# A relational graph layer: rows made unique per tile of 128 edges instead of per pair of 256, with the two scatters of a pair one after the other

## The reference

```python
h = maximum(layernorm(x), 0)                      # no scale, no shift
S = h[src]                                        # one row for each edge
for r in (0, 1):
    t = relu(S @ W_rel[r].T + b_rel[r])
    msgs = where(rel == r, relu(t @ W_rel[r].T + b_rel[r]), msgs)
agg = segment_sum(msgs, dst, num_segments=50000)  # sum the messages of each destination
gates = agg @ W_ih.T + b_ih + b_hh                # i, f, g, o
c = sigmoid(i) * tanh(g)
hn = sigmoid(o) * tanh(c)
y = relu(hn @ W1.T + b1); y = relu(y @ W2.T + b2)
out = x + y @ W3.T + b3
```

## Time and profile before

| | us |
|---|---|
| median of 3 runs | 2441.94 |
| the profiled execution | 2442.41 |
| its span | 2440.8 |
| TensorE busy | 2137.6 (88%) |
| VectorE busy | 1795.0 (74%) |
| ScalarE busy | 1632.9 (67%) |
| GpSimd busy | 1188.1 (49%) |
| DMA, mean moved | 163 GB/s |

### The profile page before, as it was taken

One profiled execution on the slowest core, in us unless ns is written; L12 is line 12 of the kernel. 1 busy time (PEld: TensorE's weight loads), 2 busy tenths in 40 slices (PEclk: granted clock), 3 DMA queues, 4 the chain that ended last, 5 costly groups with the idle time before them and its releaser, 6 DMA issues.

```text
span 2440.8 us, 51857 instructions
## 1 busy us (share of the span) xinstructions
PE 2137.6 (88%) x14224; PEld 1411.5 (58%) x14225; DVE 1795.0 (74%) x4311; ACT 1632.9 (67%) x3366; POOL 1188.1 (49%) x917
## 2 busy tenths in 40 slices
PE   6858677767999999999999999999999999899997
PEld 5747565644665666665666566566666666444543
DVE  7547555555877778777777877787887877688885
ACT  2447555546777777777777777777777777566663
POOL 0037777775555555555555555555555543200000
PEclk7569988889999999999999999999999999999998
DMA  9946555556788888888888888888888887878786
GB/s 388 425 144 101 93 96 96 95 107 121 132 158 162 165 163 161 156 152 156 164 166 161 159 152 153 160 165 164 160 158 151 161 155 141 184 174 185 192 186 142
DMA packets 400606, 396.90 MB, mean 163 GB/s; under 512 B 263738, under 2 KB 343158, under 8 KB 394360
## 3 DMA queue, kind: packets, MB, share of 16 engines
q0 software_dynamic: 91200, 157.34, 39.8%
q1 hardware_dynamic: 306788, 238.12, 37.4%
q10 hardware_dynamic: 2516, 0.14, 0.1%
HBM read 185.88 MB, written 156.97 MB: 140 GB/s over the span
## 4 chain that ended last, share of the span: by engine, by line
PE 63%; issue 13%; ACT 10%; DMA 5%; POOL 4%; DVE 1%; SPq 1%; another core or an unknown queue 1%; POOLq 0%; ACTq 0%; DVEq 0%
PE bank L1472 30%; PE bank L1419 8%; PE bank L1486 5%; PE bank L1455 4%; PE bank L1438 4%; PE bank L1401 4%; DMA agg<-summed,scatter_idx 3%; PE bank L1511 3%; POOL agg L667 2%; POOL xg L651 2%; DMA a_lo<-row_lo 2%; ACT count_tmp L739 2%; ACT summed L727 2%; ACT tcell L786 2%; PE bank L1311 2%
## 5 line engine op out<-in xcount | busy, mean ns | idle before, releaser
L667 POOL DMA_INDIRECT agg<-summed,scatter_idx x400 | 638.2, 1596 | 676.5 <-DVE scatter_idx L1147 507.7
L1472 PE MATMUL bank<-a_hi,ihT 128*128 128x512 f16 x2400 | 716.8, 380 | 19.7 <-DMA a_lo<-row_lo 19.2
L651 POOL DMA_INDIRECT xg<-in_x,src_ring x400 | 453.6, 1134 | 269.1 <-DMA src_ring<-src_slot 137.3
L1472 PE MATMUL bank<-a_lo,ihT 128*128 128x512 f16 x1200 | 456.3, 380 | 0.0
L1472 PEld LDWEIGHTS bank<-a_hi,ihT 128*128 128x128 f16 x2400 | 234.4, 98 | 233.3 <-issue 26.6
L1438 PE MATMUL bank<-relT,h_hi 128*128 x1600 | 320.5, 275 | 0.0
L1419 PE MATMUL bank<-s_hi,relT 128*128 128x256 f16 x1600 | 305.3, 287 | 0.0
L1401 PE MATMUL bank<-ident,xn 128*128 128x128 f32 x800 | 132.1, 290 | 190.2 <-ACT xn L760 97.2
L675 POOL DMA_DIRECT2D y<-in_x x100 | 133.8, 1347 | 297.0 <-DVE y L1205 275.7
L1073 DVE SCALAR_TENSOR_TENSOR s_lo<-bank,s_hi 128x512 f16<-128x512 f32 x200 | 137.8, 689 | 161.4 <-ACT s_hi L733 140.3
L733 ACT ACTIVATE s_hi<-bank 128x512 f16<-128x512 f32 x200 | 119.7, 598 | 195.5 <-PE bank L1401 157.2
(11 more groups left out here) (197 smaller groups left out, 4718.9 us busy)
## 6 DMA issues: line engine op xcount, KB each, us to landing
agg_in<-agg SPq DMA_DIRECT2D x100, 512.0 KB
y<-in_x POOLq DMA_DIRECT2D x100, 512.0 KB, 6.5
out<-y SPq DMA_DIRECT2D x100, 512.0 KB
agg<-zeros SPq DMA_DIRECT2D x24, 2112.0 KB, 15.8
dst_ring<-dst_rows SPq DMA_DIRECT2D x200, 128.0 KB
xg<-in_x,src_ring POOLq DMA_INDIRECT x400
agg<-summed,scatter_idx POOLq DMA_INDIRECT x400
src_ring<-src_slot SPq DMA_DIRECT2D x200, 1.0 KB
```

The costliest lines, as they stand in the source:

```text
L651: nc.gpsimd.indirect_dma_start(out=xg[:, k.slot(8), t, :], out_offset=None, in_=x[:, :], in_offset=bass.IndirectOffsetOnAxis(ap=src_ring[: ...
L667: nc.gpsimd.indirect_dma_start(out=agg[:, :], out_offset=bass.IndirectOffsetOnAxis(ap=scatter_idx[:, k.slot(8), t:t + 1], axis=0), in_=sum ...
L1472: last = nc.tensor.matmul(N_C[c % 2][:, 0:UNIT], lhs, rhs, start=i == 0, stop=i == len(todo) - 1)
```

## The change

For pairs of the joint part (`both`) the indices are made unique within each tile and not within the pair. The block (tile 1 with 0) is no longer compared, counted or multiplied. The two scatters of such a pair may now hit the same row, so GpSimd issues the first, waits until it has landed, and then issues the second. One of the two gathers of the step is moved between them.

```diff
+        def rows_beside(k, t):
+            return slice(2 * t, 2 * t + 1) if k.both else same_span(t)
+        def all_rows(k):
+            return slice(0, SAME_BLOCKS, 2 if k.both else 1)
 ...
             def step(at):
-                k = at + 8
-                if k.within(PAIRS):
+                to_load, to_add = at + 8, at - 4
+                if to_load.within(PAIRS):
+                    k = to_load
                     pool.wait_ge(src_loaded[k.slot(8)], 16 * (k.turn(8) + 1))
                     wait_from(pool, normed, k.n - 7)
                     pool.sem_inc(gathers_cleared, 1)
-                    for t in range(2):  (the gather of tile t)
+                    gather(k, 0)
+                    if not to_add.both:
+                        gather(k, 1)
-                k = at - 4
-                if k.within(PAIRS):
+                if to_add.within(PAIRS):
+                    k = to_add
                     pool.wait_ge(idx_ready, k.n + 1)
 ...
                     pool.wait_ge(summed_ready, k.n + 1)
                     wait_from(pool, scattered, k.n * 32)
                     pool.sem_inc(scatters_cleared, 1)
-                    for t in range(2):  (the scatter of tile t)
+                    scatter(k, 0)
+                    if not k.both:
+                        scatter(k, 1)
+                if to_load.within(PAIRS) and to_add.both:
+                    gather(to_load, 1)
+                if to_add.within(PAIRS) and to_add.both:
+                    k = to_add
+                    pool.wait_ge(scattered, k.n * 32 + 16)
+                    pool.sem_inc(scatters_cleared, 1)
+                    scatter(k, 1)
 ...
@@ counts (ScalarE): both operands
-                        same_before[:, k.slot(2), same_span(t), :]
+                        same_before[:, k.slot(2), rows_beside(k, t), :]
@@ equal (VectorE)
-                                                       dst_ring[:, k.slot(2), 0:(t + 1) * P],
+                                                       dst_ring[:, k.slot(2), (t * P if k.both else 0):(t + 1) * P],
@@ equal_before (VectorE): all three operands
-                    same_before[:, k.slot(2), :, :]
+                    same_before[:, k.slot(2), all_rows(k), :]
@@ sums (TensorE)
-                    for t in range(to, 2):
+                    for t in range(to, to + 1 if k.both else 2):
```

More of the change, by code:

```diff
@@ L665, in step @@
                     pool.sem_inc(scatters_cleared, 1)
-                    for t in range(2):
-                        nc.gpsimd.indirect_dma_start(
-                            out=agg[:, :],
-                            out_offset=bass.IndirectOffsetOnAxis(ap=scatter_idx[:, k.slot(8), t:t + 1], axis=0),
-                            in_=summed[:, k.slot(4), t, :], in_offset=None, compute_op=ALU.add).then_inc(scattered, 16)
+                    scatter(k, 0)
[8 more added lines that the diff above has]
+                    scatter(k, 1)
                 k = at.unit - 3
@@ L1131, in equal_before @@
                     dve.wait_ge(same_ready, k.n + 1)
[L1132 removed]
+                    rows = all_rows(k)
+                    nc.vector.tensor_tensor(same_before[:, k.slot(2), rows, :], same[:, k.slot(2), rows, :], earlier[:, rows, :],
                                             ALU.mult).then_inc(same_before_ready, 1)
```

22 lines of the change are left out of this document (13 added, 9 removed).

## The result

The changed kernel takes 2535.0 us (median of 4 runs, 2521.6 to 2546.3), the kernel before on the same chip 2443.6: a ratio of 1.0376, 95% interval [1.0345, 1.0407], 92 us slower. The forecast was 2428 us with a range of 2402 to 2460. Both numbers lie outside it. The nearest of the rivals is D, 2538 us, to which I had given a chance of 0.10. The execution that was profiled is the longest of the four (2546.28 us, span 2544.6).

A forecast was written before the change was run, and what follows sets the result against it. The prediction took a path through ScalarE's copy L727, TensorE's register load and the transposes as the bound. Terms -5 - 15.6 + 0 + 2 + 4.4 = -14.2 us, from 2442.4 to 2428 us; range 2402 to 2460.

The forecast's parts named there:

- D: Joint part: GpSimd's loop of landings becomes the bound, 22.6 us for two steps, 2538 us; chance 0.10.
- What bounds the kernel: Joint part: the path runs from ScalarE's copy L727 through 1.64 us of register load to the transposes; sums lie beside it.
- rival A: TensorE in the joint part: the removed sum matmuls count in full, -31.5 us, giving 2401 us; chance 0.10.
- Steps 1 and 2: Joint pairs: two sum matmuls fewer on TensorE, -5 us; ScalarE's second count reading 128 columns, not 256, -15.6 us.
- Step 4: GpSimd's wait between a joint pair's scatters: loop of landings 20.2 us in two steps of 21.0, so cost 0.
- The sign of being wrong that I had given for D: GpSimd, joint part: in most steps the second scatter's landing and not scatter_idx releases GpSimd.
- Step 5: Joint part: y's load slides some 2.5 us, SyncE's queue absorbs it; 2 us in all.
- Step 6: Tail from 2096 us: later y and one more landing in front of it, +4.4 us, bounds 2.2 to 10.
- B: Joint part: y's slide reaches TensorE through SyncE's store, transpose and a_lo; 31 us, net +17, 2459 us; chance 0.15.
- C: Tail costs 10 us and the counts bring only part of 15.6: between -7 and 0, about 2439 us; chance 0.13.

The follow-up runs named there:

- experiment 11: Kernel before with the two sum matmuls across a joint pair's tiles left out, register load kept behind the sums; ratio 1.000 to the kernel before.
- experiment 9: Kernel before with TensorE's register load of the relations moved behind the first two chunks in joint steps; 2339.2 us, ratio 0.9624.
- experiment 2: Changed kernel without the wait between scatters; tile 1 of joint pairs is added to a tensor of its own; 2418.2 us, ratio 0.9951 to the kernel before.
- experiment 1: Changed kernel's GpSimd order and waits, with the comparisons, counts and sums of the kernel before; 2530.8 us, ratio 1.0431 to the kernel before.
- 6, y first: Changed kernel with y's load issued right behind the odd step's first scatter, ahead of the moved gather and the wait; 2527.0 us, ratio 1.0354.
- 7, store later: Changed kernel with SyncE's store of y moved behind the transpose of the high rows; 2565.7 us, ratio 1.0565 to the kernel before.
- 8, agg free: Changed kernel with SyncE's steps written out and its load of agg waiting only for its quarter's scatters; 2583.9 us, ratio 1.0561.
- 10, load later: Changed kernel with TensorE's register load of the relations moved behind the first two chunks in joint steps; ratio 1.0461 to the kernel before.
- 14, half scatters: Changed kernel with each joint scatter adding only 64 of 128 rows, all waits kept; 2448.6 us, ratio 1.0072 to the kernel before.
- experiment 5: Kernel before with only y's load moved behind the next pair's gathers; 2469.8 us, ratio 1.0167.
- experiment 3: Kernel before with the changed GpSimd order and wait between scatters in odd steps only; ratio 1.0138.
- experiment 13: Kernel before with each joint scatter adding only 64 of 128 rows; 2473.6 us, ratio 1.0175.

## Why the prediction was wrong

**What bounds the kernel: right.** The path that ran through the register load and not through the sums was the unusual claim, and it is shown from both sides: four sums change nothing (experiment 11, so rival A falls), the load moved brings 91 us (9).

**Steps 1 and 2: right in kind, a little too large.** Forecast -5 and -15.6, together -20.6; measured for the reduction alone -12 (experiment 2). The 5 us were the half of a bound, and experiment 11 puts them at 0, within 5 us either way; then about 12 are left of the 15.6 of the count.

**Step 4 is the step that failed.** It took landings of 4.1 and 5.2 us and a restart of 0.4, so 20.2 us for the loop of four, 0.8 less than the steps take, and from that a cost of 0. In the rows above the landings are 4.99, 3.82, 4.58 and 6.29, 1.1 us more in sum than my 18.6, and the restart is 0.81 to 0.83 each time, 1.7 us more in sum than my 1.6. That is 22.9 for 20.2. But these rows are one long stretch. Read scatter by scatter over the joint part (600 to 2050 us, means in us, in the order odd first, odd second, even first, even second; "landing last" counts the first scatters of a pair that start within 0.95 us of the landing before them, "copy last" the others that start within 1.1 us of the end of their copy):

| kernel | four landings | in sum | landing to next start, in sum | landing last | copy last |
|---|---|---|---|---|---|
| changed | 3.81, 4.56, 5.41, 4.80 | 18.6 | 3.9 | 94 of 128 | 15 |
| 1, waits alone | 3.81, 4.71, 5.37, 4.77 | 18.7 | 3.9 | 93 of 128 | 18 |
| 6, y first | 3.72, 4.76, 6.28, 3.95 | 18.7 | 3.6 | 126 of 130 | 2 |
| 7, store later | 3.82, 4.05, 7.33, 3.97 | 19.2 | 3.5 | 110 of 128 | 1 |
| 8, agg free | 3.80, 4.58, 4.59, 4.61 | 17.6 | 5.8 | 71 of 124 | 38 |
| 10, load later | 3.88, 4.16, 5.27, 4.83 | 18.1 | 4.7 | 87 of 127 | 24 |
| 14, half scatters | 3.17, 3.36, 4.51, 4.20 | 15.2 | 6.1 | 53 of 136 | 80 |

In the mean the four landings are the 18.6 us of my forecast. The term that was mis-sized is the restart: 0.81 us at the median, 3.3 for four instead of 1.6. For it I had a row of 0.88 behind a landing in the tail, and took a value nearer to the gap between two issues, 0.30, which is no restart at all.

With it the loop is 21.8 us, 0.5 above the 21.37 of two steps. That is some 34 us over 73 units, and not all of the loss; the remaining 0.7 us or so of a unit is in the 34 of 128 first scatters that start later than that: 15 wait for their copy, which comes at the end of TensorE's and ScalarE's step, and for 19 neither is in reach (most of them are the same pairs in several kernels; why wasn't looked into). The sign of being wrong that I had given for D, a landing as the releaser in most steps, is there, but the loop and the other engines' steps end last in turn. That the thing GpSimd had idled for was scatter_idx was a misreading; it was the copy L727, at the end of the path of a step.

A landing took anything from 3.6 to 7.1 us (experiment 1), and my cost of 0 compared two means: in each step the later side sets the time. In all it is 22.60 - 21.37 = 1.23 us for each of 73 units, 90 us.

Rival D had this mechanism, this loop (22.6) and this time. Part of that is luck: it made 22.6 out of even landings of 6.4 us and a restart of 0.4, where 5.41, 4.80 and 0.81 were measured. It was wrong in one link too: it let the copy L727 wait. ScalarE doesn't wait for a scatter in the changed kernel between 700 and 1900 us. The chain goes from the landings through y's load and SyncE, which has agg, y, a_hi, dst_ring and a_lo in one order, and through TensorE; no experiment cut this whole way, and those that eased one link of it (6, 7, 8, 10) gained nothing.

The Trainium skill ("DMA: Bandwidth & Descriptors", section Anatomy of one DMA) fits a DMA from GpSimd as about 2.0 us plus its bytes over 436 GB/s. For one tile's 128 KB this gives an estimate of 2.3 us for a landing. No landing in the joint part was that short (3.6 to 7.1 us in experiment 1), so for an accumulating scatter among other transfers the measurement decides; by the page's figure and the restart measured here the loop would be 12 to 13 us, an estimate again, and no danger.

**Step 5 failed as well, and would have turned the sign alone.** I priced the slide of y at 2 us because SyncE seemed to have 6.9 us free. Experiment 5 measures 41 us for it, experiment 3 measures 34 for the odd wait alone. Less 12 for the reduction, either is a kernel slower than before. I had read the free time in SyncE's queue but not what that queue is in step with: a_hi's slide pushes dst_ring and a_lo, and y's transfer then runs beside other transfers and beside TensorE's register load. In the changed kernel this price isn't paid on top: to take the slide away gives nothing (6), because then the loop alone holds the steps. What TensorE sees of it all between 700 and 1900 us is 50.6 us more of gap ahead of the transposes, 14.0 more of waiting for a_lo and the stretches at the lower clock, less some 23 us for two sums in each of 106 steps (an estimate, from the 0.108 us of one).

The same step said of SyncE's load of agg that it needs pairs one step old and so costs nothing. It waited 123 us between 700 and 1900, but taking the wait away gained nothing (8); it was carried along and not the cause.

**Step 6: about right for what it counted.** The joint part ends with the last pair's scatters and y (GpSimd's timeline):

```profile
2199.86 1.55 POOL L657 DMA_INDIRECT agg<-summed,scatter_idx  x1 [4.05 <-DMA agg<-summed,scatter_idx]
2204.32 2.01 POOL L657 DMA_INDIRECT agg<-summed,scatter_idx  x1 [2.90 <-DMA agg<-summed,scatter_idx]
2205.76 2.40 POOL L701 DMA_DIRECT2D y<-in_x  x2
```

From the last pair's first scatter to y it is 5.90 us, for 2.84 before (2107.41 - 2104.57), and y takes 8.77 us in the chain for 6.38: 5.5 us together. From the last pair's first scatter to the end it is 8.5 us in all (344.7 for 336.2), forecast 4.4 with bounds of 2.2 and 10. What I left out lies just ahead: from pair 190 to pair 199 two steps take 19.1 us before and 22.0 in the changed kernel. The first scatters of these two pairs are 98.9 us apart for 85.8, 13 us more.

**Rivals.** A: excluded (11). B: the slide does reach TensorE, at a price of 34 to 41 us where only it is there, and B's 31 was near; but a_lo, its link, brings little of that (7.5 us of waiting in experiment 5, 3.4 in experiment 3, between 700 and 1900 us), so the price was partly luck. C: the tail was about as forecast and the counts brought most of theirs, but the rest swamped both. D: happened in the main; experiment 14 shows that it is the length of the landings that costs. The chance of 0.10 was the fault: a margin of 0.8 us in 21, made of four landings and four restarts none of which a row showed for the joint part, is no margin. The landings came out in sum by a balance of errors: the odd second took 0.5 us more than I gave it, the others together as much less.

## What to carry to other kernels

When a change makes one engine wait for the landing of its own DMA, write down that engine's whole loop (landing, restart, everything in its order) and compare it with the step; if the two are within a tenth, take the loop for the bound until a measurement says otherwise, and take the restart from a row behind a landing, not from one between two issues. Compare the spread of both and not only the means: where a landing can take 3.6 or 7.1 us, each side will be the late one in some steps. And check a releaser's name against the times: the last event before a start need not be the one that was waited for. A queue's free time is no slack for a DMA as long as other engines are in step with what stands behind it. And look for small instructions that run between two stages on the engine at the bound: moving one load of 0.54 us brought more (91 us) than all the arithmetic that the change saved (12).

## What the runs showed of the hardware

- TensorE's load of two words of `pair_rel` (which the kernel keeps in SBUF) into registers takes 0.53 us at the shortest in the kernel before between 700 and 1900 us, and 0.54 at the median. In the changed kernel it takes up to 2.2 us, in experiments 9 and 13 up to 2.5 us. What it depends on is shown for the even steps: begun 0.45 us or more behind the start of the store of `out`, it took over 0.6 us in 60 of 62 cases of experiment 13 and in 18 of 19 of experiment 9; begun ahead of it or at most 0.3 us behind, in none of 34 and none of 48 (experiment 9, kernel before). So a kernel that moves less can be slower, because the moment of a load shifts. Busy DMA engines alone don't do it: in experiment 14, 125 of 136 loads stayed under 0.6 us with the DMA engines nearly all busy beside them. What lengthened the loads of the changed kernel wasn't separated. The Trainium skill ("DMA: Bandwidth & Descriptors", section Latency and other measured facts) gives a floor of about 600 ns for such a load; the 0.53 us of these rows are under it, so the measurement decides.
- GpSimd starts the next scatter 0.8 us after the landing it waited for; behind another issue it needs 0.3, and behind the end of the copy that it waited for 1.0.
- A landing of the same 128 rows took 3.6 to 7.1 us in experiment 1. In the mean it is 3.7 to 3.9 us for the first scatter of an odd step in these kernels, and up to 7.3 for the first of an even step, where other transfers stand beside it (7). Rearranging what stands around them moved time from one landing to another: the four in sum stayed between 17.6 and 19.2 us in six kernels (1, 6, 7, 8, 10 and the change).
- TensorE's granted clock fell to 1.2 GHz for single short stretches: 12 between 600 and 2060 us in the changed kernel, 39 in experiment 10, none in the kernel before. In the one shown above TensorE had stood for 1.27 and 0.34 us just before; in it twelve chunk matmuls took 4.45 us for 2.59. In a kernel that waits anyway this cost can't be told from the wait.
